# Routing of a two-mixture kernel: the first expert's list ahead of the others', choice from logits, gates on GpSimd, a first chunk of two tiles

## The reference

```python
x = x + 0.5 * moe(layernorm(x)); x = x + attention(layernorm(x)); x = x + 0.5 * moe(layernorm(x))
# moe: E = 8 experts, K = 2 choices, F = 512, C = 1280 slots for each expert
logits = xf @ Wg;  probs = softmax(logits);  top_vals, top_idx = top_k(probs, 2)
# slot of a (choice, token): how many earlier ones, first all first choices, chose the same expert
keep = loc < C
gates = top_vals * keep;  gates = gates / max(gates.sum(-1), 1e-9)
hid = gelu(slots @ W_in[:, :F]) * (slots @ W_in[:, F:]);  out = hid @ W_out
y = sum over the two choices of out[expert, slot] * gate
```

## Time and profile before

| | us |
|---|---|
| median of three runs | 1670.18 |
| lowest, highest | 1659.63, 1670.6 |
| profiled execution | 1654.51 |
| its span, first to last instruction | 1652.8 |
| PE busy | 1448.0 (88%) |
| DVE busy | 1022.9 (62%) |
| ACT, POOL busy | 713.0, 677.1 |

### The profile page before, as it was taken

How to read it: one execution, slowest core, us unless ns; L and a number is a source line. 1 busy time by engine, 2 the same in 40 slices (tenths; PEclk the granted TensorE clock), 3 DMA queues, 4 the chain that set the end, 5 groups by cost and what they waited for, 6 DMA issues and landing times. The chain is left out here.

```text
span 1652.8 us, 25100 instructions
## 1 busy us (share of the span) xinstructions
PE 1448.0 (88%) x8712; PEld 1084.4 (66%) x8712; DVE 1022.9 (62%) x2547; ACT 713.0 (43%) x1114; POOL 677.1 (41%) x639
## 2 busy tenths in 40 slices
PE   4399999999636799999999999999865999999994
PEld 3288888899635455555555555555544998888884
DVE  6665556555265677777777778885365555655551
ACT  5233333333122155655656566565552333333331
POOL 1245655663332433333333332234204455565533
PEclk9599999999867789999999999999886999999997
DMA  9434445553267936666666578452163444444425
GB/s 312 131 91 88 78 97 100 103 99 37 32 198 217 255 122 166 171 162 161 179 161 181 149 185 259 136 162 82 60 216 91 84 97 97 101 75 86 97 33 134
DMA packets 125558, 218.25 MB, mean 132 GB/s; under 512 B 20232, under 2 KB 86280, under 8 KB 122312
## 3 DMA queue, kind: packets, MB, share of 16 engines
q1 hardware_dynamic: 88824, 165.56, 34.5%
q0 software_dynamic: 30720, 42.62, 16.5%
q10 hardware_dynamic: 5904, 8.66, 1.7%
HBM read 130.56 MB, written 90.14 MB: 134 GB/s over the span
## 5 line engine op out<-in xcount | busy, mean ns | idle before, releaser
L1933 ACT ACTIVATE a_wts<-a_s_psum 128x1024 f32<-128x1024 f32 (+1 forms) x384 | 300.8, 809 | 181.5 <-PE a_s_psum L2050 179.3
L855 POOL DMA_INDIRECT sums<-e_res,e_sum_row x160 | 253.5, 1584 | 289.2 <-ACT e_res L976 263.6
L1809 DVE CUSTOM_DVE_ANT_0 a_m_psum<-a_m_psum,mask 128x128 f32<-128x128 f32 (+3 forms) x512 | 249.1, 502 | 129.4 <-PE a_m_psum L2025 121.7
L2025 PE MATMUL a_m_psum<-a_kp,a_qp 96*128 96x512 f32 (+2 forms) x768 | 287.2, 407 | 27.1 <-DVE a_parts L1809 11.4
L2025 PEld LDWEIGHTS a_m_psum<-a_kp,a_qp 96*128 96x128 f32 x768 | 147.5, 195 | 146.1 <-DVE a_parts L1809 62.2
L242 POOL DMA_INDIRECT e_slots<-normalized,e_token x160 | 164.4, 1028 | 179.9 <-DVE e_token L577 126.3
L964 ACT ACTIVATE e_act_a<-e_a_psum 128x512 f32<-128x512 f32 (+1 forms) x192 | 101.3, 528 | 278.0 <-PE e_a_psum L1040 278.0
L1757 POOL TENSOR_SCALAR_AFFINE_SELECT a_wts<-a_wts 128x512 f32<-128x512 f32 x128 | 78.2, 634 | 333.7 <-ACT a_wts L1933 333.7
L2050 PE MATMUL a_s_psum<-a_qp,a_kp 97*128 97x512 f32 (+2 forms) x768 | 209.9, 355 | 0.4 <-ACT a_wts L1933 0.2
L898 DVE TENSOR_TENSOR e_hid<-e_act_a,e_g_psum 128x512 f32<-128x512 f32 (+1 forms) x192 | 114.7, 597 | 147.2 <-PE e_g_psum L1040 146.5
L1057 PE MATMUL e_o_psum<-e_w_hi,e_h_hi 128*128 128x256 f32 x640 | 182.6, 285 | 0.0
(11 more groups left out here) (263 smaller groups left out, 2546.2 us busy)
## 6 DMA issues: line engine op xcount, KB each, us to landing
packs<-x_res SPq DMA_DIRECT2D x48, 512.0 KB, 5.8
e_w_raw<-in_W_in SPq DMA_DIRECT2D x16, 1024.0 KB, 6.6
a_qp<-packs SPq DMA_DIRECT2D x16, 1024.0 KB, 7.7
a_kp<-packs SPq DMA_DIRECT2D x16, 1024.0 KB, 13.6
e_w_raw<-in_W_out SPq DMA_DIRECT2D x16, 512.0 KB, 8.6
normalized<-r_xn SPq DMA_DIRECT2D x16, 512.0 KB, 3.7
sums<-x_res SPq DMA_DIRECT2D x2, 4096.0 KB, 16.4
x_res<-sums SPq DMA_DIRECT2D x8, 1024.0 KB, 11.8
```

Of the source, the lines that this page charges most:

```text
L855: nc.gpsimd.indirect_dma_start(sum_dram, bass.IndirectOffsetOnAxis(ap=sum_row[:, at:at + 1], axis=0), res[j][:], None, bounds_check=last_r ...
L1809: nc.vector.tensor_tensor_reduce(products, products, c["mask"][:, QC - width:], 1.0, MASKED, ALU.add, ALU.max, top).then_inc(max_read, 1)
L1933: nc.scalar.activation(wts[(u * NS + s) % 2][:, j, 0:w], s_ps[q % 2][:, 0:w], ACT.Exp).then_inc(weighed, 1)
L2025: nc.tensor.matmul(m_ps[bank((n, h, z))][:, 0:stream], qp[n % NB][0:PACK, h, qt * P:(qt + 1) * P], kp[n % NB][0:PACK, h, part * QC:part * ...
```

## The change

`choose` works on the logits themselves: it takes maxima of `lg`, masks the first choice by adding a large negative number, and writes its masks as bf16 at once. The exponentials are taken afterwards (`centre`, `weigh`), from differences to the maximum and to the second value. `keep`, the kept weights, their sums and the gates are computed by POOL, with one reciprocal on DVE. The base of each expert's slots (1280 times its number) comes into the rank matmul as a 65th row of `earlier`, so that the slot is a number over all experts. The number of a list entry carries the tile times 128.

The list is made in two passes. The first has the 10 columns of expert 0 alone (`is_first`, `first_valued`: 20 columns) over all 64 pairs; its tokens are made at once and POOL may gather. The second has the other 70 columns. The masks of places are all kept (four buffers). POOL gathers 2 tiles in `route` instead of 4. Expert 0 works in chunks of 256, 512 and 512 slots (`FIRST_CHUNKS`), with the transposes of chunk 1 after step 1 of up(0) and those of chunk 2 after step 1 of up(1). Of the low part of expert 0's weights, two of three parts are taken in `route`, the third in `experts` behind the first split (`first_rest`); SP's load of expert 1's weights waits for it.

```diff
-CHUNKS = [(0, 512), (512, 512), (1024, 256)]
+FIRST_CHUNKS = [(0, 256), (256, 512), (768, 512)]
-FIRST_TILES = CHUNKS[0][1] // P
+FIRST_TILES = FIRST_CHUNKS[0][1] // P
+FIRST_PARTS = 2
...
                 def choose(i):
                     dve.wait_ge(logits_done, (i + 1) * H // CH)
-                    link(nc.vector.reduce_max(den[:], lg[i], AX.X))
-                    nc.vector.tensor_tensor(prob[:], lg[i], wide(den[:]), ALU.subtract).then_inc(centred, 1)
-                    dve.wait_ge(powered, i + 1)
-                    link(nc.vector.reduce_sum(den[:], prob[:], AX.X))
-                    link(nc.vector.reciprocal(den[:], den[:]))
-                    link(nc.vector.tensor_tensor(prob[:], prob[:], wide(den[:]), ALU.mult))
...
+                    for k, scores in enumerate((lg[i], left[:])):
+                        link(nc.vector.reduce_max(top[:, k, tiles], scores, AX.X))
+                        link(nc.vector.tensor_tensor(pick[:], scores, wide(top[:, k, tiles]), ALU.is_ge))
                         link(nc.vector.tensor_tensor(pick[:], pick[:], rank, ALU.mult))
                         link(nc.vector.reduce_max(rk[:, k, tiles], pick[:], AX.X))
+                        nc.vector.tensor_tensor(hot_bf[:, k, tiles, :], rank, wide(rk[:, k, tiles]), ALU.is_equal).then_inc(hot_ready, 1)
...
+                def centre(i):
+                    nc.vector.tensor_tensor(prob[i][:], lg[i], wide(top[:, 0, tiles]), ALU.subtract).then_inc(centred, 1)
+                    nc.vector.tensor_tensor(behind[i][:], top[:, 1, tiles], top[:, 0, tiles], ALU.subtract).then_inc(centred, 1)
+                def weigh(i):
+                    dve.wait_ge(powered, (i + 1) * 2)
+                    link(nc.vector.reduce_sum(den[:], prob[i][:], AX.X))
+                    link(nc.vector.reciprocal(best[:, 0, tiles], den[:]))
+                    nc.vector.tensor_tensor(best[:, 1, tiles], behind[i][:], best[:, 0, tiles], ALU.mult).then_inc(weighed, 1)
                 choose(0)
+                centre(0)
                 choose(1)
+                centre(1)
+                weigh(0)
...
+                pool.wait_ge(slots_summed, 1)
+                link(nc.gpsimd.tensor_scalar(keep[:], rk[:], float(CAP), None, ALU.mult))
+                link(nc.gpsimd.tensor_tensor(keep[:], keep[:], slot[:], ALU.add))
+                nc.gpsimd.tensor_scalar(keep[:], keep[:], float((EXP + 1) * CAP), None, ALU.is_lt).then_inc(kept_ready, 1)
...
+                for k in range(TOPK):
+                    nc.gpsimd.tensor_tensor(gates[:, :, k], kept[:, k, :], sums[:], ALU.mult).then_inc(gates_ready, 1)
...
+                dve.wait_ge(kept_ready, 1)
+                link(nc.vector.scalar_tensor_tensor(flat(column), tile_i[:], 1.0, flat(keep), ALU.add, ALU.mult))
+                link(nc.vector.tensor_scalar(columns[:], flat(column).unsqueeze(2).to_broadcast([P, NK, 2]), -1.0, None, ALU.add))
+                nc.vector.tensor_tensor(paired(is_first[:]), pairs(c["spots"][:, 0:ST], NK, ST),
+                                        along(columns[:], NK, ST), ALU.is_equal).then_inc(is_made, 1)
...
+                late_columns(0)
+                dve.wait_ge(piece_read, PIECES)
+                tokens(slice(0, ST), first_ps[:, 0:ST], first_ps[:, ST:])
+                for z in range(1, PIECES):
+                    late_columns(z)
+                rows_and_choices(slice(0, ST), 1)
+                for z in range(FIRST_PARTS):
+                    weights_rest(z)
+                dve.wait_ge(piece_read, 2 * PIECES)
+                tokens(slice(ST, SLOTS), late_ps[:, 0:LATE], late_ps[:, LATE:])
+                rows_and_choices(slice(ST, SLOTS), 2)
...
 (experts, PE)
-                        up(0, {1: 1, 3: 2})
+                        up(0, {1: 1})
...
-                    up(1)
+                    up(1, {1: 2} if first else {})
...
 (experts, DVE)
+                def first_rest():
+                    for a, b in W_PARTS[FIRST_PARTS:]:
+                        nc.vector.tensor_tensor(w_lo[0][:, a:b], w_raw[:, a:b], w_hi[0][:, a:b].bitcast(F32), ALU.subtract).then_inc(w_rest, 1)
+                slots_lo(0, 0, FIRST_CHUNKS)
```

More of the change, by code:

```diff
@@ L570, in _ @@
-                dve.wait_ge(listed, 1)
-                lane, tile = listed_ps[:, 0:SLOTS], listed_ps[:, SLOTS:]
-                first, second = (a[:] for a in held["choice"])
-                link(nc.vector.tensor_scalar(second, tile, float(NT + 1), None, ALU.is_ge))
-                link(nc.vector.tensor_scalar(row[:], tile, float(P), -float(P), ALU.mult, ALU.add))
-                link(nc.vector.tensor_tensor(row[:], row[:], lane, ALU.add))
-                link(nc.vector.scalar_tensor_tensor(row[:], second, -float(TOK), row[:], ALU.mult, ALU.add))
@@ L577, in _ @@
-                nc.vector.tensor_scalar(held["token"][:], row[:], 0.0, None, ALU.max).then_inc(list_ready, 1)
-                link(nc.vector.tensor_scalar(none, tile, 0.0, None, ALU.is_equal))
-                link(nc.vector.tensor_tensor(none, none, c["aside"][:], ALU.mult))
-                link(nc.vector.tensor_tensor(held["sum_row"][:], row[:], none, ALU.add))
-                link(nc.vector.tensor_scalar(first, second, -1.0, 1.0, ALU.mult, ALU.add))
-                dve.wait_ge(w_split, len(W_PARTS))
@@ new lines, in late_columns, with tokens @@
+                    dve.wait_ge(is_made, z + 2)
+                    nc.vector.tensor_tensor(paired(valued[z % 2][:, :, LATE:]), paired(is_column[z % 2][:]),
+                                            along(number[:, kts, :], N, LATE), ALU.mult).then_inc(column_made, 1)
+                def tokens(cols, lane, tile):
+                    link(nc.vector.tensor_copy(numbers[:, cols], tile))
+                    link(nc.vector.tensor_tensor(row_i[:, cols], numbers[:, cols], lane, ALU.add))
+                    nc.vector.tensor_scalar(held["token"][:, cols], row_i[:, cols], TOK - 1, None, ALU.bitwise_and).then_inc(list_ready, 1)
@@ new lines, in rows_and_choices @@
+                def rows_and_choices(cols, ready):
+                    first, second = (a[:, cols] for a in held["choice"])
+                    tile = numbers[:, cols]
+                    link(nc.vector.scalar_tensor_tensor(none[:, cols], tile, 0.0, c["aside"][:, cols], ALU.is_equal, ALU.mult))
+                    dve.wait_ge(list_ready, ready)
+                    link(nc.vector.tensor_tensor(held["sum_row"][:, cols], none[:, cols], held["token"][:, cols], ALU.add))
+                    link(nc.vector.tensor_scalar(second, tile, float((NUMBER0 + NT) * P), None, ALU.is_ge))
+                    link(nc.vector.tensor_scalar(first, second, -1.0, 1.0, ALU.mult, ALU.add))
@@ L928, in body @@
                         slots_lo(e, 2)
-                    between = {0: gates}
                     if more:
-                        between[1] = lambda: weights_rest(0)
+                        between[0 if first else 1] = lambda: weights_rest(0)
                     hidden(1, between)
@@ L968, in results @@
                     def results(ci):
-                        c0, n = CHUNKS[ci]
+                        c0, n = chunks[ci]
                         if ci == 0:
@@ L991, in body @@
                         weights_high(0)
-                    gelu(1)
+                    gelu(1, {1: lambda: slots_hi(e, 2, chunks)} if first else {})
                     if more:
@@ L1044, in up @@
                             if f in between:
-                                transposes(e, u, i, between[f])
+                                transposes(e, u, i, between[f], FIRST_CHUNKS, FIRST_SLOTS_IN)
                     def down(ci):
-                        c0, n = CHUNKS[ci]
+                        c0, n = chunks[ci]
+                        if first and ci == 0:
+                            pe.wait_ge(w_rest, NW)
                         h = (u * NC + ci) % 2
```

208 lines of the change are left out of this document (118 added, 90 removed).

## The result

| | before | changed |
|---|---|---|
| median, same chip, 20 runs each | 1666.94 us | 1657.54 us |
| lowest, highest | 1659.53, 1670.6 | 1648.88, 1667.71 |
| ratio, 95% interval | | 0.9948 (0.9928 to 0.9967) |
| profiled execution, span | 1654.51, 1652.8 | 1657.3, 1655.3 |

The change saves 9.4 us, 0.5%; 1661.4 was predicted, with a gain of 8.8. The two profiled executions stand the other way round: the one of before lies 12 us under its median, the one of the changed kernel on it.

A forecast was written before the change was run, and what follows sets the result against it. VectorE's path, then GpSimd's gathers and drain, bound the route block ahead of a busy TensorE. Per round 9.6 - 2.7 - 2.5 = 4.4, twice 8.8: 1645.7 profiled, 1661.4 us on the median's scale; range 1646 to 1669.

The forecast's parts named there:

- last mask of the choice: In route, VectorE's choice shrinks from 17 steps to 11 up to the one-hot masks; last mask starts at 41.39, 2.25 us sooner.
- mask for expert 0: In route, VectorE's first list mask starts at 47.3 instead of 50.38, 3.1 us sooner, with 0 to 0.3 waiting for `keep`.
- The block's end and the start of the experts: VectorE, not GpSimd, ends the route block, at 67.3 instead of 74.98; first expert matmul at 70.4, 9.6 us sooner.
- The late pieces: Three VectorE mask pieces for the late list of 70 columns, 1.43 us each, the last waiting for TensorE, until 61.9.
- The first list pass: TensorE's 64 matmuls of 20 columns for expert 0's list, bound by weight loads at 0.13 us each, ending at 56.5.
- The gates' DMA: Gathers in route wait for it; inputs end on GpSimd at 51.5 to 53.4, so it lands at 56 to 57.9.
- The pause: In expert 0 after 24 matmuls, TensorE waits 2.7 us (0.2 to 3.4) for chunk 1's tiles, the fourth landing at 78.2.
- The clock's setback: The pause restarts TensorE's clock rise in expert 0: some 5 us more at half speed, costing 2.5 us a round.
- a rival of 0.20: The pause in expert 0 leaves the clock alone: gain 6.9 a round, 13.8 in all, 1656.4 us; chance 0.20.
- The rival of starving gathers: VectorE's gapless late list holds GpSimd's gathers in route; drain at 71.5, gain 0.1 a round, 1670 us; chance 0.12.
- the slower rival: Waits keep the clock low through the interrupted first expert's first two chunks: -6.0 a round, 1682 us; chance 0.04.
- The shift to the median: The three-run median, 1670.2, lies 15.7 us above the profiled 1654.5; added to the forecast 1645.7, giving 1661.4.

The follow-up runs named there:

- w64 run: Changed kernel with 16 added matmuls, loading only 64 of the 128 weight columns, behind each of the four pieces of the first list pass; 1654.75 us.
- tiles4 run: Changed kernel, but GpSimd gathers four tiles in the route block instead of two; 1631.7 us, ratio to before 0.9868.
- tiles4_gates run: Changed kernel with four tiles gathered in the route block and the last two gate steps on VectorE instead of GpSimd; 1652.9 us, ratio to before 0.9905.
- the changed kernel's second profile: Changed kernel unaltered, run and profiled again on another chip; 1643.5 us against 1652.9 for before, ratio 0.9938.
- the first set: Runs on the chip where before took 1652.9 us: both kernels again (changed 1643.5), expert 1's weight load behind chunk 1's tiles (1628.5), four tiles gathered in route (1631.7).

## Why the prediction came true, and where it erred

| step | predicted | measured |
|---|---|---|
| last mask of the choice | 41.39 | 41.33 |
| mask for expert 0 | 47.3 | 47.89 |
| first pass ends | 56.5 | 54.46 |
| list ready | 57.2 | 55.8 |
| first gather | 58.1 | 59.30 |
| GpSimd's drain closes | 64.8 | 63.9 |
| VectorE's drain closes | 67.3 | 66.4 |
| first expert matmul | 70.4 | 69.6 |
| pause | 2.7 | 3.5, 3.2 |
| setback of the clock | 2.5 | 2.5, 2.8 |
| net, a round | 4.4 | 4.5 |

**The block's end and the start of the experts** were right in kind, VectorE for GpSimd, and 0.9 and 0.8 us off. The late pieces took 1.55 us each instead of 1.43, but they were not held up by a slow first pass: they ended at 61.1 instead of 61.9, with one wait of 0.86 us for TensorE in them, and the rest ran as priced. The mask for expert 0 in front of them came 0.6 late: VectorE waited 0.49 for GpSimd's `keep`, where 0 to 0.3 was priced.

**The first list pass: the step that failed.** It was sized at 0.13 us a matmul, from the counting matmuls of the earlier trace rows, and TensorE was called its bound. It took 27 ns a matmul, 0.58 us a piece instead of 2.1, and waited for VectorE before each. Eight narrow, strided loads said nothing of full ones; the w64 run shows both sides. The prediction had named a first pass faster than its weight loads as a sign against itself, and a TensorE without pauses there as a sign for itself; both went against it. The low clock did not matter either. The error cost nothing: the tokens came 1.4 us sooner than predicted, and the gathers did not, since they waited for something else. The Trainium skill, TensorE: Matmul & The Clock Gate, section Weight-path perf modes — Fast Weight Load (FWL) and DoubleRow, says that weights of 128 columns, not of 32-bit floats, are loaded in a faster way; the trace agrees, 27 ns against 53 ns for half the columns, and this was the rule to weigh, instead of the 107 ns of the same page's LDWEIGHTS section that the prediction quotes.

**The gates' DMA** was expected beside the list or before it, 56 to 57.9, and let GpSimd go at 59.3: the two gate steps took 2.29 us on GpSimd where VectorE worked beside it, the DMA was issued at 53.95, and its landing let GpSimd go 5.3 us later. The prediction had given the drain room for that, and it had: with two gathers GpSimd's drain closes 2.5 us before VectorE's. With four gathers the room is gone (the tiles4 run: 1.0 us on the path), and moving the gate steps brings the first matmul 0.6 us sooner (the tiles4_gates run, 28.6 instead of 29.2), a gain that its time, taken under lags, does not show.

**The pause** has the predicted cause: the gather issued behind the load of expert 1's weights landed after 5.8 us (5.6 were taken from the earlier trace rows), and with the load behind it after 2.8. It was 0.8 longer (0.5 in the second round) because TensorE came sooner, 74.0 instead of 75.5: it had started 0.8 earlier, and the clock rose after 3.0 us, inside the 24 matmuls that were priced at the low clock throughout. The two errors of the sum, a start that was earlier than predicted and a longer pause, cancel; that is luck.

**The clock's setback** was a term with a rival of 0.20 that it is nothing. Filling the pause kept the clock at 1.00 and made the stretch 2.5 and 2.8 us shorter. The prediction had a rise that starts again; in the trace the clock had risen at 72.6 and fell back at 76.0, and it rose again at 82.9. The rival of starving gathers has fallen with the tiles4 run (1.8 us at most for a gather); the slower rival, a clock low through the first two chunks, has too, in the changed kernel's second profile, where it is at 1.00 from 84 on.

**The shift to the median** (15.7 us from the profile of before to its median) was treated as a plain offset. By the lengths of the expert stages it is most likely the lags. That it still worked is in part luck: the changed kernel's profiled execution, which had them, took 1657.3 us, not the 1645.7 of the sum; what held is the difference of the medians, 9.4 us both in the first comparison and on the chip without lags.

## What to carry to other kernels

When a list is made in pieces so that its first part can be used early, look at what the early consumer starves next: here the second chunk's tiles, whose gathers and whose competing load now fell into the same 8 us. A load that nobody needs for 20 us should stand behind the transfers that are needed in five. And do not price matmuls with few moving columns from a row with narrower weights. When an edit pays on one chip and not on another, look in the trace at the instants of the semaphores, and not only at the ends of the instructions.

## What the runs showed of the hardware

- TensorE's signal of finished work can come 1 to 9.6 us late, in any of these kernels, and ScalarE and VectorE start only with it: nine profiles show it 16 to 29 times each, five (the first of before, and the four of the first set) never, with every signal 13 to 15 ns behind its matmul. In the first expert the held signals come within 0.8 us of the gathers' last packet. It cost before 10 us of 371 in each expert stage, and it absorbed what an edit had gained for TensorE: 15 us of gain over the changed kernel on one chip, none that can be told on another.
- A matmul with 128 weight columns and 20 moving ones takes 27 ns at 1.2 GHz, with 64 weight columns 53 ns, and with 64 strided weight columns and one moving 120 ns.
- Two small GpSimd steps (32 elements) took 2.29 us beside VectorE's 1.2 us mask steps, where three of 64 elements took 0.3 to 0.5 each beside others.
- An indirect gather behind the change of block landed in 2.7 to 3.4 us with no load near it (4.4 where a VectorE step stretched it), and in 5.8 to 6.6 when 1.5 MB of weights were asked for within about a microsecond before or after it.
- The clock rose 2.8 to 5.0 us after the first expert matmul in the changed kernel and its variants, and 3.6 to 6.2 us after it in the three profiles of before.
